# VectorE takes the two narrow key groups of each half, and the second gate's inverse becomes an event of its own

## The reference

```python
S = jnp.einsum('hid,hjd->hij', K, Q) * SCALE
S = jnp.where(delta < 0, -jnp.inf, S) + decay
C = jax.nn.softmax(S, axis=-1)
attn = jnp.einsum('hij,hjd->hid', C, V)
...
logits = h @ gate_w.T                              # router
scores = jnp.sqrt(jax.nn.softplus(logits))
_, topk_idx = jax.lax.top_k(scores + bias[None, :], K)
...
si = jax.nn.silu(h @ sg.T) * (h @ su.T)            # shared expert
si = jnp.clip(si, -SWIGLU_LIMIT, SWIGLU_LIMIT)
shared = si @ sd.T
```

## Time and profile before

| | us |
|---|---|
| median of 3 runs | 3596.42 (3596.02 to 3599.44) |
| the profiled execution | 3624.72 |
| its span, first to last instruction | 3622.9 |
| mean granted TensorE clock | 0.943 of full |

### The profile page before, as it was taken

One profiled execution on the slowest core, in us unless ns is written; L12 is line 12 of the kernel. 1 busy time (PEld: TensorE's weight loads), 2 busy tenths in 40 slices (PEclk: granted clock), 3 DMA queues, 4 the chain that ended last, 5 costly groups with the idle time before them and its releaser, 6 DMA issues. The chain is left out here.

```text
span 3622.9 us, 61678 instructions
## 1 busy us (share of the span) xinstructions
PE 3221.6 (89%) x20358; PEld 1667.9 (46%) x20366; DVE 2086.9 (58%) x5798; ACT 1218.9 (34%) x2823; POOL 1753.1 (48%) x988
## 2 busy tenths in 40 slices
PE   4667999989999999999999899999999998687998
PEld 2334444444444444444444444444444444255775
DVE  6843444466646664666466645664566466755555
ACT  3661333333333333333233323332333233311111
POOL 5740354455545553555355535553555355643322
PEclk8878999999999999999999999999999998888999
DMA  5862200121111001010101010101010100205996
GB/s 186 302 255 74 91 30 4 45 73 53 57 69 48 18 16 54 16 36 14 56 16 36 13 54 19 36 13 54 19 36 13 53 19 13 73 4 172 258 254 149
DMA packets 121810, 253.64 MB, mean 70 GB/s; under 512 B 38749, under 2 KB 39389, under 8 KB 118929
## 3 DMA queue, kind: packets, MB, share of 16 engines
q1 hardware_dynamic: 77152, 200.36, 16.4%
q0 software_dynamic: 44048, 49.26, 5.3%
q10 hardware_dynamic: 288, 0.00, 0.0%
HBM read 144.61 MB, written 202.16 MB: 96 GB/s over the span
## 5 line engine op out<-in xcount | busy, mean ns | idle before, releaser
L967 POOL TENSOR_TENSOR a_first_probs<-a_first_probs,a_probs 128x2048 f32<-128x2048 f32 (+3 forms) x320 | 1031.5, 3224 | 1010.8 <-ACT a_probs L1047 928.4
L1205 DVE CUSTOM_DVE_ANT_0 a_unused<-a_ps_ring,a_work 128x512 bf16<-128x512 f32 (+3 forms) x1536 | 779.0, 555 | 897.9 <-PE a_ps_ring L1535 894.0
L1047 ACT ACTIVATE a_probs<-a_ps_ring 128x512 f32<-128x512 f32 (+3 forms) x1280 | 508.2, 473 | 365.0 <-PE a_ps_ring L1569 256.0
L1559 PE MATMUL a_ps_ring<-a_k_t,a_q_t 32*128 32x512 f32 (+3 forms) x3072 | 436.7, 536 | 78.1 <-DVE a_row_max L1205 52.6
L1535 PE MATMUL a_ps_ring<-a_q_t,a_k_t 32*128 32x512 f32 (+3 forms) x3072 | 393.8, 552 | 14.5 <-DVE a_row_max L1205 12.5
L978 POOL DMA_INDIRECT d_slots<-a_rows,a_place_i x349 | 350.0, 1003 | 71.9 <-issue 61.2
L1559 PEld LDWEIGHTS a_ps_ring<-a_k_t,a_q_t 32*128 32x128 f32 x3072 | 156.4, 185 | 281.3 <-issue 130.4
L1535 PEld LDWEIGHTS a_ps_ring<-a_q_t,a_k_t 32*128 32x128 f32 x3072 | 145.2, 190 | 283.4 <-issue 257.4
L974 POOL TENSOR_TENSOR a_attn_t<-a_attn_t,a_sum_inv 128x512 f32<-128x512 f32 x64 | 83.2, 1301 | 379.8 <-DVE a_sum_inv L1220 379.8
L1047 ACT ACTIVATE a_first_probs<-a_ps_ring 128x512 f32<-128x512 f32 x256 | 135.8, 606 | 381.9 <-PE a_ps_ring L1569 356.9
L1582 PE MATMUL a_ps_heads<-a_probs,a_values 128*32 128x512 f32 (+3 forms) x2560 | 261.6, 481 | 0.0
(11 more groups left out here) (283 smaller groups left out, 4325.9 us busy)
## 6 DMA issues: line engine op xcount, KB each, us to landing
d_hidden<-e_hidden SPq DMA_DIRECT2D x8, 2048.0 KB
d_normed_t<-e_normed_t SPq DMA_DIRECT2D x8, 2048.0 KB, 11.8
a_work<-d_normed_t SPq DMA_DIRECT2D x7, 2048.0 KB
a_hidden<-d_hidden SPq DMA_DIRECT2D x56, 256.0 KB, 2.7
out<-a_hidden SPq DMA_DIRECT2D x56, 256.0 KB
d_slots<-a_rows SPq DMA_DIRECT2D x32, 408.8 KB, 5.9
x_rows<-d_slots SPq DMA_DIRECT2D x32, 408.8 KB
x_w_gate<-w_gate SPq DMA_DIRECT2D x16, 512.0 KB
```

The source lines that it names most:

```text
L967: nc.gpsimd.tensor_tensor(total_of, total_of, probs_of(m)[:, :, 0:width], ALU.add).then_inc(added, 1)
L1047: nc.scalar.activation(probs_of(m)[:, h, 0:width], score_bank(m, h)[:, 0:width], ACT.Exp).then_inc(exp_done, 1)
L1205: nc.vector.tensor_tensor_reduce(unused[:, (HG * k + h) % N_UNUSED, 0:width], row_bank(k, h)[:, 0:width], decay[:, at:at + width], 1.0, NE ...
L1559: nc.tensor.matmul(score_bank(m, h)[:, 0:width], q_t[st.g][dims, j * P:(j + 1) * P], k_t[st.g][dims, i0:i0 + width], start=True, stop=False)
```

## The change

Two parts. First, the adds of slots 2, 3, 10 and 11 (`NARROW`) go from POOL to DVE (`add_narrow`), after the row maxima of their slot, with a semaphore of their own, `narrow_added`; POOL keeps six adds a step (`WIDE`). ACT, before it writes a `probs` buffer again, waits for whichever engine adds that group, and PE's `sum_probs` waits for DVE's last add of the half. Second, the reciprocal of a gate becomes `invert_gate`. For gate 0 it stays where it was; for gate 1 it stands one slot earlier, after the row maxima of slot 9, while the products and the clip stay behind slot 10. The late gates behind the last step keep their order.

```diff
-ADDS = N_GROUPS - 2
-EARLY_ADDS = HALF_GROUPS - 1
+NARROW = (2, 3, 10, 11)
+WIDE = tuple(m for m in range(N_GROUPS) if m not in NARROW and GROUPS[m][1] > 0)
...
+INVERT_GATE_AT = ((7, 1), (9, 1))
 GATE_AT = {True: ((7, 1), (10, 1)), False: ((7, 1), (10, 1))}
...
             def add_probs(st, m):
-                if j == 0:
+                if m not in WIDE:
                     return
...
-                wait_from_1(pool, added, ADDS * st.s + later(m))
+                wait_from_1(pool, added, len(WIDE) * st.s + WIDE.index(m))
...
                     if k >= 0 or not st.first:
-                        act.wait_ge(added, ADDS * st.s + k + 1)
+                        of = group_of_later(k) if k >= 0 else group_of_later(k + N_GROUPS - 2)
+                        s = st.s if k >= 0 else st.s - 1
+                        if of in WIDE:
+                            act.wait_ge(added, len(WIDE) * s + WIDE.index(of) + 1)
+                        else:
+                            act.wait_ge(narrow_added, len(NARROW) * s + NARROW.index(of) + 1)
...
+            def add_narrow(st, m):
+
+                half, j, i0, width = shape(m)
+                n = NARROW.index(m)
+                dve.wait_ge(exp_done, ITEMS * st.s + HG * (m + 1))
+                if m - 1 in NARROW:
+                    wait_apart(dve, narrow_added, len(NARROW) * st.s + n, passed)
+                else:
+                    wait_apart(dve, added, len(WIDE) * st.s + WIDE.index(m - 1) + 1, passed)
+                total_of = first_probs[half][:, :, HALF - width:HALF]
+                nc.vector.tensor_tensor(total_of, total_of, probs_of(m)[:, :, 0:width], ALU.add).then_inc(narrow_added, 1)
...
+            def invert_gate(x, m, inner_t):
+
+                dve.wait_ge(gate_e_done, MC * x + m + 1)
+                nc.vector.reciprocal(inner_t[:, m, :], inner_t[:, m, :]).then_inc(gate_inverted, 1)
+
             def gate(x, m, inner_t, gate_up, use, chain):
...
-                dve.wait_ge(gate_e_done, MC * x + m + 1)
-                chain.done(nc.vector.reciprocal(inner, inner))
-                chain.wait()
+                dve.wait_ge(gate_inverted, MC * x + m + 1)
...
+                if (m, after) == INVERT_GATE_AT[1]:
+                    invert_gate(x, 1, inner_t)
...
                     if st.rows:
                         row_maxima(st.s + 1, m)
+                    if m in NARROW:
+                        add_narrow(st, m)
...
             def sum_probs(s, half, use):
-                pe.wait_ge(added, ADDS * s + (ADDS if half else EARLY_ADDS))
+                pe.wait_ge(narrow_added, len(NARROW) * s + sum(1 for m in NARROW if half or m < HALF_GROUPS))
```

9 lines of the change are left out of this document (7 added, 2 removed).

## The result

The changed kernel takes 3567.1 us (median of 4 runs, 3559.1 to 3570.6), the kernel before, run beside it, 3597.9 (3596.0 to 3599.8). The ratio is 0.9912, its 95% interval 0.9898 to 0.9926. The forecast was 3562.6, its range 3543 to 3585. The profiled execution of after took 3559.1 us, 8 less than the median. That of before took 3624.7, 27 more than its median, and was not made beside this one. So the two traces differ by 66 us where the medians differ by 31; what follows compares places in the traces first and asks for the rest later.

What follows compares the result with a forecast made beforehand. PE bounds the kernel, waiting 97.9 us before `down` in 28 places. Terms: -35.3 chain, +5.5 slot 11's add, +1 variance, -5 clock, sum -33.8 us: 3596.4 becomes 3562.6, range of 8 in 10 3543 to 3585.

Steps and rivals of the forecast that it cites:

- The chain: DVE in slot 10 before `down`: reciprocal out, 1024-column add in, 2.33 us instead of 3.59; gain 35.3 us in 28 steps.
- The moved reciprocal: Gate 1's reciprocal, 1.75 us, between the row maxima of slots 9 and 10: covered by DVE's idle time, cost nothing.
- Rival (b): Before slot 10: the count meets POOL's multiplication, row maxima 0.7 us later in 28 steps, 20 us, total 3583; chance 0.09.
- The adds in slots 2 and 3: DVE adds of 1.23 and 0.69 us behind row maxima, covered by idle time before the next ones; cost nothing.
- The add in slot 11: Ahead of the second `down`'s L1378: PE waits 0.36 us in 14 steps, 5.0 us; with one g = 0 case, 5.5.
- The variance: L1243 comes 0.72 us later and may meet POOL's add of slot 1; 1 us taken in all.
- Rival (d): Slots 0 and 1, g = 1 and 3: POOL's adds block DVE at the variance; 45 us slower, 3608; chance 0.05.
- The clock: First `down` behind PE's wait: the clock's fall costs 39 us over 28 steps; 5 us of it expected back.
- Rival (a): First `down`: the clock comes back in most steps; half of 39 us gives 3548, all of it 3529; chance 0.09.
- The last step: No row maxima, POOL behind, 5.3 us wait before `down`; counted like the other steps, 1.26 us gained.
- the cover: DVE's 1.91 us of idle time before slot 10's row maxima, said to hide the moved reciprocal; without it up to 49 us.
- Rival (c): At `down`: wait not shortened, as the add takes 2.37 us or time returns at PE's next row-maxima wait; 3595; chance 0.07.

Runs made afterwards that it cites:

- the kernel with the late adds and no slip: Kernel with the late adds, gate 1's reciprocal behind slot 10's count except for g = 0, where it stays ahead; 0.9778 of the kernel before.
- the run with slot 11's add alone: Against the whole change: only slot 11's add on DVE, at the step's end; slots 2, 3, 10 on POOL, reciprocal still moved; 0.9871 of the kernel before.
- the kernel with the late adds: Against the whole change: DVE adds slot 10 behind the places in slot 11, and slot 11 at the step's end; 0.9826 of the kernel before.
- the last kernel: Late adds of slots 10 and 11 only, reciprocal placed by the step, slot 10's add moved behind the first `down`; 3525.6 us, 0.9744 of the kernel before.

## Why the prediction was right, and where it was not

The forecast, -33.8 us, met the first pair's -30.8. In two later sets, on chips of their own, the whole change gains 17 and 11 us, the second of them just beyond the slow end of the range (13 to 55 us below the 3597.9 of the first pair). The mechanism that it named, the shorter chain before `down`, is right in every trace; the sum held in one comparison of three.

**The chain.** Right to a few hundredths: adds of 1.22 and 0.69 us (1.23 and 0.69 forecast), product 0.42 (0.43), clip 0.29, together 2.73 instead of 3.98 us, 1.25 a step (1.26). PE's wait before `down` is 2.11 at the median and 55 us in all (2.2 and 62). The adds and the products are these groups (count, busy us, mean ns of one, idle before):

```profile
L1216 DVE TENSOR_TENSOR a_first_probs<-a_first_probs,a_probs 128x1024 f32<-128x1024 f32 x64 | 78.1, 1220 | 0.0
L1216 DVE TENSOR_TENSOR a_first_probs<-a_first_probs,a_probs 128x512 f32<-128x512 f32 x64 | 44.0, 687 | 0.1
L1393 DVE TENSOR_TENSOR a_inner_t<-a_gate_up,a_inner_t 128x256 f32<-128x256 f32 x56 | 28.5, 510 | 3.1
```

To price an add of a size that the trace doesn't show by a line through two sizes that it does was good enough. That the first product and the clip shrink only if POOL's add of slot 11 goes was in the working, and the run with the inverse alone shows how much hangs on it: 1.08 us a step.

**The moved reciprocal.** Here the prediction failed. It said: "Behind the reciprocal it starts at about 1539.6, with the add over, and takes 0.5." The start was right (the same 2.4 us behind slot 9's row maxima), the length was not; it is the second line here (least, median, greatest in ns), which had 494/1465/1474 in the earlier trace rows:

```profile
engine op xcount: duration ns min/median/max, first and last start us, forms
L1315 DVE TENSOR_TENSOR a_is_top<-a_experts_row,a_late_top_at x28: 494/2024/2340, 720.8 to 3101.1; 128x384 bf16<-128x384 f32 x28
```

Rival (b) named this meeting, with the condition that L1295 come after the start of POOL's multiplication. The count met it while starting 0.28 to 0.59 us before, inside the scatter that stands directly ahead. The 0.6 us that the prediction held against the rival were there, and were just not enough (the last section has the edge). The slip was 0.44 us, not 0.7, and in 14 to 19 steps by the trace, not 28; its price on the path, by the two runs that take it away, is 0.43 us each, 8 us for the 18 steps of the first trace, not 20. So the term "cost: nothing" should read 8, and rival (b) was half true.

**The adds in slots 2 and 3.** By themselves they fit, as forecast, and the kernels with and without them come out alike in time (0.9826 and 0.9820; 0.9778 and 0.9770, each pair on two chips). That a gap in DVE's stream would appear beside them on three chips, and slot 2 take some 5 to 8 us more in all, was in no term.

**The add in slot 11.** Forecast 0.36 us in 14 steps, 5 us. L1401 now ends 0.05 us before the projection that wants its bank, where it was 0.50, and PE starts it 0.14 us later in 13 of the 26 steps, 1.8 us. The step was right and its size nearly three times too large: L1401 was pushed 0.58 us and not 0.72, and there were 0.44 to spare and not 0.36, since PE takes the bank up 0.06 us behind DVE's end and not 0.14.

**The variance.** With g = 1 and 3 it stays 0.17 us long in all traces of the whole change, ahead of POOL's add by 0.3 to 2.0. Rival (d) is false. The 1 us is too small to be seen.

**The clock.** The 5 us did not come. With a wait of 2.1 us no first `down` of 28 is short, and the stretch behind the wait, which had 0.59 in the earlier trace rows, has a granted clock of 0.50, the lower of the two levels (1.2 GHz) throughout:

```profile
1526.50:1530.00 3.50, 3.44 (x4) 1.18 (x4) 1.98 (x14) 0.00 (x0) 0.00 (x0) 0.50 0.02 5
```

Rival (a) was right in kind for the kernels that came after: with a wait of 0.97 us and no slip, 17 of 28 are at 2.4 GHz and 1.8 us shorter each. The prediction's full price, 39 us, was read from step 13, whose first `down` (3.39 us) is one of the shortest; over the 28 steps of the trace of before it is 48.

**The last step** won 3.0 us (5.3 to 2.3) where 1.26 was counted. That is 1.7 more.

With what was measured, -35 + 8 + 1.8 - 1.7 = -27 us. The first pair gained 4 us more than this, the second and third 10 and 16 less. The traces put the difference at slots 0 to 3, at the loop's return and behind the last step, in both directions, and none of it is in the prediction's terms. What decides it from one chip or execution to the next stays open. That the forecast came within 5 us owes something to errors that cancel in part (the cover, too good by 8; the clock, by 5; slot 11 and the last step, too bad by 4 and 2) and to luck with the chip or the execution. Rival (c), "the change doesn't shorten the wait", falls; but its second form, the time coming back at PE's next wait for row maxima, is where the price of the slip stands: 52.6 us of such waits before, 62.4 after, 50.5 in the kernel with the late adds and no slip.

## What to carry to other kernels

When an instruction is moved into another engine's idle time, check not only that it fits, but what the instruction pushed by it will now stand beside: here one with two inputs in SBUF was held through a whole POOL operation that it would have cleared by its start and length. An operation that nobody waits for does not belong into a chain that the bottleneck waits for, however short it is; behind the next instruction that must wait anyway it costs nothing, and the two late adds moved so brought 29 us more at this place, where the whole change had brought 26. Measure a change of under 1% on more than one chip before its size is believed.

## What the runs showed of the hardware that I had not expected

- A DVE instruction with two SBUF inputs can be held by a POOL one that, by its recorded start, comes later. Over all traces here, the count L1315 (L1295 before; its line is another in some kernels) starts 148 times with a scatter of POOL in flight and the multiplication directly behind it. The 134 that start 0.26 to 0.60 us ahead of the multiplication are held until its end, 2.0 to 2.34 us instead of 0.50; the 14 that start 0.60 to 0.75 ahead are free. The edge is sharp, within 5 ns of 0.60: the count of step 13 above stands 0.59 ahead and is held, and this one, step 25 of the whole change's third trace, is not:

```profile
2626.29 0.99 POOL L981 DMA_INDIRECT d_slots<-a_rows,a_place_i  x1 [0.16 <-issue]
...
2626.68 0.50 DVE L1315 TENSOR_TENSOR a_is_top<-a_experts_row,a_late_top_at 128x384 bf16<-128x384 f32 x1
...
2627.29 1.31 POOL L977 TENSOR_TENSOR a_attn_t<-a_attn_t,a_sum_inv 128x512 f32<-128x512 f32 x1
```

That is the main reason why equal programs slip in 14, 18 and 19 steps. Where POOL stood idle ahead of the multiplication, as in step 12 of before, the count starts 0.17 us ahead, takes 0.50, and the multiplication 1.46 instead of 1.31:

```profile
1454.59 0.50 DVE L1295 TENSOR_TENSOR a_is_top<-a_experts_row,a_late_top_at 128x384 bf16<-128x384 f32 x1
...
1454.76 1.46 POOL L974 TENSOR_TENSOR a_attn_t<-a_attn_t,a_sum_inv 128x512 f32<-128x512 f32 x1 [1.45 <-DVE a_sum_inv L1220]
```

The rule of the Trainium skill cited in the prediction, that whichever starts first holds the other off, fits this second case by the recorded starts, and the first only if POOL's claim is laid 0.60 us before the multiplication's recorded start. The measurement decides; whether it is the multiplication or the scatter, 0.40 us after its own start, that lays it, these runs don't show.
- Gaps of 0.4 to 1.1 us in the stream of one engine, in which its bookkeeping instructions pause too: 12 on ACT in the trace of before, none in the first trace after, 20 on ACT and 36 on DVE in another of the same program. They stand at fixed places of the program, move when instructions are added, and differ by chip or execution. One of 0.5 us, at slot 10 with g = 0, shows in no list of waits as remote. On a chain that PE waits for, as at L1326 in the run with slot 11's add alone, one costs as much as the change gains.
- At the loop's return PE stood still 2.2 to 2.5 us in four of six batches of the trace before, and 0.9 to 1.0 in the first three of the first trace after. There the granted clock didn't fall with the shorter stand, and the next output projection took 3.65 us instead of 4.6 to 5.3; together 3 us a batch, though the change is elsewhere. But the length of the stand alone doesn't decide it: in the kernel with the late adds the projection took 3.65 us behind a stand of 2.6, and in the last kernel 5.35 behind one of 1.4.
- The granted clock before `down`: none of 28 at 2.4 GHz with a wait of 2.1 us, 4 to 17 of 28 with one of 1.0, and more of them where the row maxima ahead don't slip (12 to 17 against 4 to 8, on different chips).
